# Attention 1 of a two-layer model: queries gathered by quarters, down blocks beside raw scores, the last projection inside the loop

## The reference

```
# layer 0, feed-forward
g = einsum('th,ih->ti', xf, gate_w) * gate_s      # 256 -> 704
u = einsum('th,ih->ti', xf, up_w) * up_s
hdn = silu(g) * u
out = einsum('ti,hi->th', hdn, down_w) * down_s   # 704 -> 256
...
# layer 1, attention: 32 heads of 8, 8 key groups, 16 sequences of 128 tokens, causal
q = (Q @ w_q.T).reshape(B, S, G, HG, HD)
scores = einsum('bnghd,bmgd->bnghm', q, k) / sqrt(8)
attn = softmax(where(causal & mask, scores, -inf))
out = einsum('bnghm,bmgd->bnghd', attn, v) @ w_o.T + b_o
x = x + tanh(g_xattn[1]) * out
...
# layer 1, feed-forward: eight experts, top-1 routing with capacity
```

## Time and profile before

| | us |
|---|---|
| median of three runs | 1509.68 (1508.69 to 1513.91) |
| the profiled execution | 1504.61 |
| its span, first to last instruction | 1502.7 |
| PE busy | 1347.6 (90%) |
| DVE busy | 1151.5 (77%) |
| ACT busy | 982.2 (65%) |
| POOL busy | 812.0 (54%) |

### The profile page before, as it was taken

The page is one execution under the profiler, slowest core; times in us unless marked ns, Lnnn a source line. Parts: engine busy times, 40 slices in busy tenths (PEclk is TensorE's granted clock), DMA queues, the critical chain, the costliest instruction groups (busy, mean ns, idle before and its releaser), DMA issues. The chain is left out here.

```text
span 1502.7 us, 29308 instructions
## 1 busy us (share of the span) xinstructions
PE 1347.6 (90%) x11216; PEld 1146.1 (76%) x11216; DVE 1151.5 (77%) x2269; ACT 982.2 (65%) x2168; POOL 812.0 (54%) x801
## 2 busy tenths in 40 slices
PE   0687999999999999999999997799877999985994
PEld 0576999999999999999999996577643555554994
DVE  8799888888888888988888898533346777764564
ACT  4797878778778778778877775422115665662772
POOL 5777566556566565666565443200105766663672
PEclk9799999999999999999999999899987999995997
DMA  3101100100100000000001000443445101004563
GB/s 106 57 8 29 35 3 16 37 15 11 27 15 15 22 16 15 22 16 27 11 15 53 2 1 1 137 54 38 82 73 82 26 16 58 16 15 144 201 210 133
DMA packets 63546, 69.98 MB, mean 47 GB/s; under 512 B 6736, under 2 KB 56112, under 8 KB 63280
## 3 DMA queue, kind: packets, MB, share of 16 engines
q1 hardware_dynamic: 60800, 60.74, 16.0%
q0 software_dynamic: 2432, 7.34, 1.4%
q10 hardware_dynamic: 176, 0.04, 0.0%
HBM read 55.56 MB, written 12.34 MB: 45 GB/s over the span
## 5 line engine op out<-in xcount | busy, mean ns | idle before, releaser
L849 POOL TENSOR_TENSOR RB<-YS,M 128x512 bf16<-128x512 f32 x128 | 162.2, 1267 | 254.7 <-DVE YS L709 254.7
L536 ACT ACTIVATE QT<-B,sm 128x256 f32<-128x256 f32 x256 | 131.5, 568 | 166.9 <-PE B L393 166.9
L413 PE MATMUL SS<-QT,KT 128*128 128x256 f32 x512 | 154.8, 397 | 9.6 <-DVE mx L664 9.2
L845 POOL TENSOR_TENSOR yy<-vv,half 128x12 f32<-128x12 f32 x64 | 147.1, 2298 | 5.3
L361 PE MATMUL PA<-WH,XQ 128*128 128x256 f32 x512 | 141.0, 307 | 4.9 <-ACT SQ L565 4.9
L363 PE MATMUL PA<-WL,XQ 128*128 128x256 f32 x512 | 130.0, 286 | 0.0
L683 DVE TENSOR_TENSOR QN<-QN,yy 128x512 f32<-128x512 f32 x128 | 122.3, 956 | 2.1 <-POOL yy L845 2.1
L1622 ACT ACTIVATE P<-PO,mcf 128x1024 f32<-128x1024 f32 x64 | 71.3, 1114 | 79.2 <-PE PO L1487 79.2
L664 DVE TENSOR_REDUCE mx<-SS 128x4 bf16<-128x512 f32 x128 | 88.0, 688 | 43.8 <-PE SS L405 43.8
L676 DVE TENSOR_REDUCE vv<-SQ 128x6 f32<-128x768 f32 x128 | 120.6, 942 | 0.0
L381 PE MATMUL PA<-W,XB 128*128 128x128 bf16 x1536 | 109.4, 221 | 2.7 <-POOL XB L786 2.7
(11 more groups left out here) (334 smaller groups left out, 4372.8 us busy)
## 6 DMA issues: line engine op xcount, KB each, us to landing
W<-in_w SPq DMA_DIRECT2D x16, 1024.0 KB, 8.1
Q<-qsc SPq DMA_DIRECT2D x48, 128.0 KB
WR<-in_wprojT SPq DMA_DIRECT2D x16, 256.0 KB, 3.0
K<-ksc SPq DMA_DIRECT2D x12, 256.0 KB
qsc<-T POOLq DMA_DIRECT2D x8, 384.0 KB, 4.2
X<-in_x SPq DMA_DIRECT2D x4, 512.0 KB, 5.9
CR<-in_xctxT SPq DMA_DIRECT2D x8, 256.0 KB, 2.8
RSM<-rsm_d SPq DMA_DIRECT2D x16, 128.0 KB, 4.2
```

Source lines behind the costliest of these rows:

```text
L413: pe.matmul(SS[:, 256 * z:256 * z + 256], k[:, 128 * z:128 * z + 128], q[:, 256 * z:256 * z + 256], start=True, stop=False)
L536: a.activation(QT[i % 2][:, o:o + 256], B1[:, o:o + 256], ACT.Identity, bias=col(n + "b"), scale=col(n + "w"))
L845: p.tensor_tensor(yy[j % 2][:], v_, half[:], ALU.pow).then_inc(s_rstd, 1)
L849: p.tensor_tensor(RB[i % 2][:], YS[:], M[:], ALU.subtract).then_inc(s_rb, 1)
```

## The change

Layout:
- XH and XL, one tile each over all tokens before, become four tiles each, one a quarter, allocated in turn. SG moves behind GH and GL.
- Q6 becomes [128, 4, 16, 512], quarter by quarter, so that quarter 0 lies over the parts XH/XL of token quarters 0 and 1. The tiles of att1 are ordered anew, with two unused fillers.

SP: the gather of query quarter 0 waits for `s_hd` 12 (the last use of token quarter 1) rather than 24. Quarter 1 still waits for 24. The number, size and shape of the gathers are the same.

POOL: the two stores of query quarter 0 stand ahead of the power of quarter 1, not behind it. The stores of quarter 3 move from ahead of the loop to iteration n = 12, and the first value tiles from n = 7 to n = 10.

PE and DVE: down blocks 8 to 11 leave the feed-forward stage, and down blocks 8 to 15 alternate with raw(0) to raw(7). Query quarter 2 is turned after raw(5) and projected ahead of raw(7). Quarter 3 is turned in loop iteration 8 and projected in iteration 10, its split in iterations 10 and 11. The clearing of VE and VO moves into iteration 9 and waits for the stores of quarter 2. The transposes and projections use other PSUM banks.

ACT: the wait for the stores of quarters 2 and 3 (s_qst[2], s_qst[3]) moves from the first `act_upper` (iteration 9) to the first `act_evac_out` (iteration 13), since now OTS lies over the store buffers.

```diff
@@ sp_attention_1
-            sp.wait_ge(s_hd, 24)
-            for q4 in range(2):
-                for half in range(2):
-                    sp_queries(sp, q4, half)
+            sp.wait_ge(s_hd, 12)
+            for half in range(2):
+                sp_queries(sp, 0, half)
+            sp.wait_ge(s_hd, 24)
+            for half in range(2):
+                sp_queries(sp, 1, half)
@@ pe_feed_forward_0, dve_feed_forward_0
-                if q4:
+                if q4 in (1, 2):
                     for b in range(4 * q4 - 4, 4 * q4):
@@ pe_attention_1
-            pe_down(pe, 12)
-            pe_raw(pe, 0)
-            pe_down(pe, 13)
-            pe_raw(pe, 1)
-            pe_query_turn(pe, 2)
...
+            for i in range(8):
+                pe_down(pe, 8 + i)
+                if i == 7:
+                    pe_query_proj(pe, 2)
+                pe_raw(pe, i)
+                if i == 5:
+                    pe_max_turn(pe, 0)
+                    pe_query_turn(pe, 2)
             for n in range(8, N1 + 19):
...
+                if n == 8:
+                    pe_query_turn(pe, 3)
+                if n == 10:
+                    pe_query_proj(pe, 3)
@@ act_upper -> act_evac_out
-            if i == 0:
+            if u == 0:
                 a.wait_ge(s_qst[2], 32)
                 a.wait_ge(s_qst[3], 32)
@@ dve_attention_1
+            for i in range(8):
+                dve_down(v, 8 + i)
+                if i % 4 == 3:
+                    dve_layer_root(v, 2 + i // 4)
+                if i == 7:
+                    dve_query_proj(v, 2)
+                dve_maximum_1(v, i)
+                if i == 4:
+                    dve_layer_scale(v, 2, 2)
+            dve_layer_scale(v, 2, 3)
...
+                if n == 9:
+                    dve_clear_values(v)
+                if n in (10, 11):
+                    dve_query_proj(v, 3, (n - 10,))
@@ pool_attention_1
+                if n == 10:
+                    pool_values(p, 0)
+                if n == 12:
+                    pool_query_stores(p, 3)
```

More of the change, by code:

```diff
@@ L1030, in pe_gate_up @@
                 for c in range(2):
-                    for z, (a, b) in enumerate(((GH, XH), (GL, XH), (GH, XL))):
-                        t = pe.matmul(ps_[0:m, :], a[:, w, c, 128 * n:128 * n + m], b[:, c, q], start=c == 0 and z == 0,
+                    for z, (a, b) in enumerate(((GH, XH[q4]), (GL, XH[q4]), (GH, XL[q4]))):
+                        t = pe.matmul(ps_[0:m, :], a[:, w, c, 128 * n:128 * n + m], b[:, c, :], start=c == 0 and z == 0,
                                       stop=c == 1 and z == 2)
@@ L1076, in turn_banks @@
         def turn_banks(q4):
-            return (SS[:], POa) if q4 == 2 else (B1[:], B2[:]) if q4 == 3 else PAh
+            return (SS[:], PC[:]) if q4 == 2 else (B1[:], B2[:]) if q4 == 3 else PAh
         def proj_banks(q4):
-            return (POb, PC[:]) if q4 >= 2 else PAh
+            return (POa, POb) if q4 == 2 else (SS[:], PC[:]) if q4 == 3 else PAh
         def pe_query_turn(pe, q4):
@@ L1170, in act_query_turn, with act_query_proj @@
                 a.activation(XF[:, c, 512 * q4:512 * q4 + 512], ps_, ACT.Copy).then_inc(s_qxt, 1)
-        def act_query_proj(a, q4):
+        def act_query_proj(a, q4, tis=(0, 1)):
             qs = QS2[q4 % 2]
-            if q4 == 0:
+            if q4 == 0 and 0 in tis:
                 a.wait_ge(s_kv, 4)
                 a.wait_ge(s_ks, 64)
-            if q4 >= 2:
+            if q4 >= 2 and 0 in tis:
                 a.wait_ge(s_qst[q4 - 2], 32)
-            for ti, ps_ in enumerate(proj_banks(q4)):
+            for ti in tis:
                 a.wait_ge(s_qp, 2 * q4 + ti + 1)
-                a.activation(qs[:, ti, 0, :], ps_, ACT.Copy).then_inc(s_qpa, 1)
+                a.activation(qs[:, ti, 0, :], proj_banks(q4)[ti], ACT.Copy).then_inc(s_qpa, 1)
                 a.wait_ge(s_qr, 2 * q4 + ti + 1)
@@ L1337, in build @@
         sb = sbt(att1)
-        PH1 = [sb(f"PE1{i}", [128, 2, 256], FR) for i in range(3)]
-        PL1 = [sb(f"PL1{i}", [128, 2, 256], FR) for i in range(3)]
+        WO = sb("WO", [128, 2, H])
+        VE = [sb(f"VE{i}", [128, 4, 128], FR) for i in range(2)]
+        VO0 = sb("VO0", [128, 4, 128])
         OTS = [sb(f"OTS{i}", [128, 512]) for i in range(2)]
@@ L1389, in heads_at, with of_block @@
             return b, 2 * d, slice(128 * b, 128 * b + 128)
+        def of_block(b):
+            return b // 4, slice(128 * (b % 4), 128 * (b % 4) + 128)
         def parity(p1, odd):
```

104 lines of the change are left out of this document (41 added, 63 removed).

## The result

| | before | changed |
|---|---|---|
| median | 1511.8 us (1508.69 to 1515.78, 4 runs) | 1495.5 us (1492.92 to 1498.34, 4 runs) |
| profiled execution, its span | 1504.61, 1502.7 | 1492.92, 1491.1 |
| mean granted clock | 0.961 | 0.968 |

The ratio is 0.9891 with a 95% interval of 0.9859 to 0.9924. The forecast was 16.1 us. A second set of executions, timed beside the last experiments, gave 1495.81 against 1510.27, ratio 0.9896 [0.9869, 0.9923].

A forecast was written before the change was run, and what follows sets the result against it. The prediction took a chain of waits mostly through PE to bound the kernel and followed the start of raw(16). Its terms summed to 16.1 us earlier there, taking the median from 1509.7 to 1493.6 us, range 1485 to 1502.

The forecast's parts named there:

- Gather of quarter 0: Ahead of raw(0): twelve DMAs take 18.1 us, in by 1063 to 1065, so PE's 8.93 us wait goes.
- PE to raw(7): From 1069.12, down blocks, raw scores, turn and projection of quarter 2 sum to 35.9 us; raw(7) ends at 1105.0.
- DVE late next: At raw(8), PE waits 3.5 us for DVE's maximum of raw(7), behind add, root and split of quarter 2.
- Loop head at full clock: Iterations 8 to 12, followed by instruction: raw(11) at 1118.5, raw(12) at 1121.6, raw(13) at 1126.4, 24 us earlier.
- The clock: Around PE's wait at raw(8), it falls at about 1108, returns at about 1117: +2.6 us at raw(13), 1129.
- Stores of quarter 3: Issued by POOL in n = 12, they land after 7.2 us, at 1137.5; ACT waits for them in n = 13.
- Sum: raw(16) starts at 1142.7, with 1.6 us added for the lower clock, against 1158.85 before: 16.1 us gained.
- Its own signs: Wrong if raw(16) is before 1137 or after 1150, Q<-MT waits show at shifted(4) or shifted(8), or later stages lose.
- Slow stores with starved maxima: Quarter 3's stores take 13.0 us or maxima of blocks 1 and 2 come late: gain 9 us, 1500.7; chance 0.13.
- Fast stores with the clock kept: Quarter 3's stores take 3.4 us and the clock holds: raw(16) at 1135.8, gain 23 us, 1486.6; chance 0.22.

The follow-up runs named there:

- gathers later, PE filled: Changed kernel with gathers of quarters 2 and 3 issued at blocks 2 to 5 and 15 useless products between raw(7) and raw(8): 1486.34 us, ratio 0.9826.
- all three edits: Changed kernel with quarters 2 and 3 gathered at blocks 2 to 5, 15 useless products after raw(7), and OTS over RQ: 1484.10 us, ratio 0.9819.
- late-gather run: Changed kernel with SP's wait before the gather of quarter 0 put back to s_hd 24: 1516.09 us, ratio 1.0029.
- the filled one: Changed kernel with 15 useless products between raw(7) and raw(8), where PE waits for DVE: 1494.83 us, ratio 0.9897.

## Why the prediction was right, step by step

| event, us from P | forecast | measured | measured, second profile | gathers later, PE filled | all three edits |
|---|---|---|---|---|---|
| raw(8) | 42.8 | 42.6 | 42.6 | 42.6 | 42.6 |
| raw(11) | 52.8, low clock not counted | 57.4 | 53.7 | 52.5 | 53.8 |
| raw(13) | 60.7, with the clock 63.3 | 64.4 | 65.1 | 59.5 | 60.8 |
| ACT's wait ends | 71.8 | 71.6 | 75.0 | 64.7 | none |
| raw(16) | 77.0 | 76.6 | 80.0 | 69.7 | 71.0 |

The forecast column is the prediction's times less 1065.68. Of the kernels in the last two columns, the clock of the first was never low between P and raw(16); that of the second was, twice for 3.4 us.

- *Gather of quarter 0.* The step holds: in the late-gather run its absence costs more than the whole gain, and given in the old order it brings 12.1 us (of 16.6 or 13.2, by the two profiles). Its size was wrong. The forecast took 1.51 us a DMA at 87 GB/s; the stretch from 1048 to 1070 moved 69 GB/s, so by estimate 131 KB takes 1.9 us and twelve take 22.8, until about P + 0.2. Raw(0) came at P + 6.3, so the error was hidden by 6 us of slack.
- *PE to raw(7).* Forecast end P + 39.3; measured start 38.2 plus 0.87 is 39.1.
- *DVE late next.* 3.5 us forecast, 3.51 measured, the same instructions in the same order.
- *Loop head at full clock.* Raw(11) and raw(12) were put at P + 52.8 and 55.9. The changed kernel has 57.4 and 60.0, the filled one, whose clock stayed up, 52.5 and 55.9.
- *The clock.* It fell where it was expected, and stayed low for 13.6 us instead of 9. The charge of 2.6 us at raw(13) was too small: between the two runs with later gathers, which differ by the filler alone, raw(13) came 4.6 us apart (P + 64.1 and 59.5). The full-clock time that it was added to, 60.7, was 1.2 us too late by the same run, which hides part of it. The prediction's reading of before was loose too: its rows put the falls at 1087.2 and 1128.2 and the last return at 1148.6, and a third low stretch of before, from 1114.5 to 1117.9, was overlooked. Not foreseen: about as much is lost without the low clock, since the maxima of block 1 then wait in the queue. The rival named that wait and priced it at 1 us or less, from 1.51 us a DMA; where it showed it was 3.5 to 3.7.
- *Stores of quarter 3.* The landing time taken was 7.2 us; it was 5.4 in one profile and up to 8.6 in the other. Their issue was 1.4 us later on the axis from P (65.2 against 63.8). The end of ACT's wait, forecast P + 71.8, was 71.6. Two errors cancel here. That the gathers in flight set this time is shown: with them moved away it was 3.0 to 3.5. The rule of the Trainium skill that the step cites ("DMA: Bandwidth & Descriptors", section on queues, rings and completion order: a semaphore's increment lands only behind the earlier writes of the same DMA engine) agrees with that, though no run separates it from plain sharing of bandwidth.
- *Sum.* 16.1 forecast for raw(16), 16.6 measured, 16.3 between the medians. That these agree to half a microsecond is partly luck: the second profile of the same kernel gives 13.2 for raw(16), the interval of the medians is 10 us wide, and the terms above are off by 1 to 2 us in both directions.
- *Its own signs.* Among what would show it wrong the prediction names a wait for Q<-MT at shifted(4). The first profile has none; the second has it, 3.69 us. So the mechanism of the forecast holds for one of the two executions that were looked into, and in the other a rival's wait stands beside it, with the total inside the forecast's bounds for raw(16) in both.
- *Rivals.* Slow stores with starved maxima is the nearest: the second profile of the changed kernel has its wait for the maxima and stores of 8.6 us, at the same median. Fast stores with the clock kept, 70.1 us to raw(16) by the prediction, is what the kernel becomes with gathers later and filler (69.7).

Left open: why twelve gathers run at 69 GB/s here. The DMA share is 0.55, as it was at 87 before. In the early gather with the old order they ran at 67, so the order of PE's work is not the cause by itself; in the late gather they ran at 71, so neither is the early start. The new layout of Q6 is common to all the slower stretches, but no run has it alone. Also open is what the order of the queues is worth on top of the early gather, and how long the clock stays low behind the same 3.51 us wait: 13.6 us in one execution and 3.4 in another of one kernel.

## What to carry to other kernels

Start a transfer from the last use of the memory that it overwrites, part by part, and only then thin out the work that covered it: here the reordering without the early gather cost 0.3%, and on top of it brought no more than 0.3%, which is not clear of noise. When a plausible cure moves the time by nothing, look in its own trace for what now waits at the same place before giving it up: the filler alone brought no gain that could be seen, its trace showed the wait for the maxima in its place, and with the gathers out of the queue as well the kernel was 0.65% faster than the changed one. Keep bulk transfers that nobody wants yet out of a queue that carries small urgent ones.

## What the runs showed of the hardware that was not expected

- A small DMA of maxima behind six gathers of 131 KB in one queue landed 12.7 us after its issue; with the gathers moved away it landed after 1.7 us.
- After PE stood for 3.51 us the clock was low for 13.6 us in one execution and for 3.4 us in another of the same kernel. Fifteen products of no use, 3.41 us, in that wait kept raw(8) to raw(10) at full speed in all three kernels that had them. Between medians they made 3.7 and 5.1 us where the gathers were later, and nothing that could be seen where they were not.
- Gathers of the same size and count moved 59 to 71 GB/s in the kernels with the new layout and 87 in a stretch of before, at DMA shares of 0.54 to 0.59.
